# A software-pipelined attention pass on one Trainium2 core: a new written order of the first pass, and the mixture's weights fetched one piece per element

## The reference, cut to what matters

```python
x = x + _L0_xattn_ref(_layernorm(x), ctx, ctx, mask, ...)   # 16 heads of 8, 77 keys, bias by distance
x = x + _L0_ffn_ref(_layernorm(x), ...)                      # the two parts below
# part 1: layer norm, 3-tap convolution over tokens, q k v, rotation of q and k,
#         causal attention with 16 heads over 128 keys, projection
# part 2: layer norm, h @ router_w, argmax over 4 experts, then for the chosen expert
#         (silu(gate) * value) @ expert_proj[e], with gate, value = split(h @ expert_wv[e])
```

## Time and profile before

| what | us |
|---|---|
| time, three runs | 3200.71, 3202.42, 3205.06 |
| median | 3202.42 |
| the profiled execution, its own time | 3210.65 |
| its span, first to last instruction | 3208.9 |
| busy in the span: PE, DVE, ACT, POOL | 2783.6, 2658.8, 2508.3, 828.6 |

### The profile page before, as it was taken

How to read it: one execution, slowest core, us unless ns; L and a number is a source line. 1 busy time by engine, 2 the same in 40 slices (tenths; PEclk the granted TensorE clock), 3 DMA queues, 4 the chain that set the end, 5 groups by cost and what they waited for, 6 DMA issues and landing times. The chain is left out here.

```text
span 3208.9 us, 78310 instructions
## 1 busy us (share of the span) xinstructions
PE 2783.6 (87%) x28057; PEld 2002.6 (62%) x28057; DVE 2658.8 (83%) x7379; ACT 2508.3 (78%) x6617; POOL 828.6 (26%) x1437
## 2 busy tenths in 40 slices
PE   6999899999999759979999997876688888888887
PEld 4666666666666536656767674334566667667665
DVE  4899898999989525459999995788599999999995
ACT  4999899999999525547777773687599998999995
POOL 1233233333333100025555541000122221222221
PEclk7999999999999669989999997998789998999997
DMA  1011311111111011101111111001200000000000
GB/s 47 26 33 33 78 33 33 33 30 31 32 33 33 14 54 42 43 22 33 35 34 35 34 33 30 1 0 32 69 10 15 15 15 15 14 15 15 15 15 8
DMA packets 176000, 91.15 MB, mean 28 GB/s; under 512 B 46243, under 2 KB 171877, under 8 KB 175619
## 3 DMA queue, kind: packets, MB, share of 16 engines
q1 hardware_dynamic: 170084, 76.85, 8.9%
q0 software_dynamic: 4096, 8.40, 0.8%
q10 hardware_dynamic: 1440, 0.90, 0.1%
HBM read 43.73 MB, written 42.36 MB: 27 GB/s over the span
## 5 line engine op out<-in xcount | busy, mean ns | idle before, releaser
L2299 DVE TENSOR_TENSOR th<-tf 128x2048 f32<-128x2048 f32 x256 | 583.5, 2279 | 12.1 <-PE p_rho L2203 8.1
L2149 ACT ACTIVATE th<-th 128x2048 f32<-128x2048 f32 x256 | 488.9, 1911 | 6.8 <-DVE th L2299 6.8
L643 ACT ACTIVATE probf<-probf,colf 128x128 f32<-128x128 f32 x1024 | 314.4, 403 | 0.0
L2203 PE MATMUL p_rho<-th,late_w_row 128*32 128x128 f32 x8192 | 301.6, 285 | 13.1 <-ACT th L2149 13.1
L613 ACT ACTIVATE prob<-prob,col 128x77 f32<-128x77 f32 x1024 | 270.0, 352 | 4.6 <-DVE col L896 4.6
L2160 ACT ACTIVATE tl<-tf 128x128 f32<-128x128 f32 x832 | 256.9, 390 | 0.0
L2203 PEld LDWEIGHTS p_rho<-th,late_w_row 128*32 128x32 f32 x8192 | 229.4, 113 | 28.3 <-ACT th L2149 17.8
L1755 PE MATMUL acc<-xnT_all,wT 128*128 128x512 f32 x384 | 181.3, 625 | 29.6 <-DVE tmax L1947 13.2
L791 PE MATMUL fp<-ident,probf 128*128 128x128 f32 x1024 | 145.0, 287 | 27.3 <-ACT ygf L650 24.6
L942 DVE TENSOR_TENSOR probf<-fs,causal 128x1024 f32<-128x1024 f32 x128 | 153.7, 1201 | 16.9 <-PE fs L779 16.9
L2264 PE MATMUL p_f<-w_pair,xm 128*128 128x128 f32 x1024 | 166.8, 330 | 0.0
(11 more groups left out here) (432 smaller groups left out, 7964.2 us busy)
## 6 DMA issues: line engine op xcount, KB each, us to landing
rows<-zeros SPq DMA_DIRECT2D x64, 256.0 KB, 2.4
cxT<-in_ctxT SPq DMA_DIRECT2D x128, 38.5 KB, 2.0
xb<-rows SPq DMA_DIRECT2D x67, 64.0 KB, 1.8
rows<-yb SPq DMA_DIRECT2D x67, 64.0 KB, 1.5
x<-in_x SPq DMA_DIRECT2D x64, 64.0 KB, 1.8
x_mid<-x SPq DMA_DIRECT2D x64, 64.0 KB, 1.5
z<-x_mid SPq DMA_DIRECT2D x64, 64.0 KB
x_next<-z SPq DMA_DIRECT2D x64, 64.0 KB, 1.5
```

What stands on the lines that cost most here:

```text
L643: last = nc.scalar.activation(scores, scores, ACT.Exp, bias=colf[s][:, 16 + HALF * hf + h:17 + HALF * hf + h])
L2149: nc.scalar.activation(b[:], b[:], ACT.Tanh).then_inc(act_done, ACT_L.did(f"t{c}.tanh", e))
L2203: last = nc.tensor.matmul(p_rho[r][ROWS * b:ROWS * (b + 1), 0:TOK], w_row[:, ROWS - 1 - a:2 * ROWS - 1 - a], tanh[:, k, :], start=(a == 0) ...
L2299: nc.vector.tensor_tensor(th[i % NT][:], tf[s][:, n * KT:(n + 1) * KT].unsqueeze(2).to_broadcast([128, KT, TOK]), tf[s][:, FEAT:FEAT + TOK ...
```

## The change

The four texts of the first pass are replaced. The steps and what they compute stay; only their order on each engine and the number of turns by which each lags are new. The first lines of the diff show all of the new PE, ACT, DVE and POOL orders.

Beside it the two transfers of all four experts' weights become four and four, one per expert, and SP no longer issues the list at e = 16 but one entry of it per element, from e = 8 on: 13 entries of `moe_loads` at e = 8 to 20 and the four convolution rows at e = 21 to 24.

```diff
+PE_A = """
+    x0b.PT@2 f0a.PV@5 f0b.S@4 f0b.PT@5 f0.qkv@3 x0b.PV@2 f0b.PV@5 x0.T x0.ygT@2 f0.ygT@5 x0.qkv fc.route@6 f0.yT@5
+    x0.yT@2 f0.o@5 x0.o@2 x0a.S x0a.PT@1 fc.rank@6 fc.T@5 f0a.S@3 x0b.S x0a.PV@1 f0a.PT@4 f0.T@2
+"""
 ACT_A = """
-    f0a.exp@5 x0.v@1 fc.xT@6 x0a.PTc@2 f0a.PTc@5 x0a.yg@2 f0b.exp@5 f0a.yg@5 f0.xT@3 x0b.PTc@2 f0b.PTc@5 x0a.exp@1
-    f0b.yg@5 x0b.yg@2 x0b.exp@1 f0.yT@5 f0.v@3 x0.xT x0.yT@2
+    f0b.yg@5 x0.xT x0a.exp@1 f0.yT@5 x0.yT@2 x0.v f0a.exp@4 x0a.PTc@1 fc.xT@5 f0b.exp@4 x0a.yg@1 f0a.PTc@4 f0.xT@2
+    x0b.PTc@1 f0a.yg@4 x0b.exp f0b.PTc@4 x0b.yg@1 f0.v@2
 """
 DVE_A = """
-    fc.eq@7 fc.first@7 f0.x@6 fc.stats@6 fc.aggr@6 x0.x@3 fc.eps@6 fc.pick@7 fc.taken@7 x0.kT@1 f0.stats@3 f0.aggr@3
-    fc.norm@6 x0.qT@1 f0.qk@4 f0.eps@3 f0b.max@5 x0a.add@1 f0.h@3 fc.slot@7 x0a.max@1 f0.norm@3 x0b.add@1 f0a.add@4
-    x0b.max@1 f0.conv2@3 f0.conv1@3 x0.stats f0.conv0@3 f0a.max@4 x0.aggr f0b.add@4 x0.eps f0.rope@3 f0.rden@5 f0.y@5
-    x0.rden@2 x0.norm x0.y@2 fc.slot_i@7 fc.max@6
-"""
-PE_A = """
-    x0b.S@1 f0a.S@4 f0a.PV@5 f0.T@3 x0b.PT@2 f0b.PT@5 f0b.S@4 x0b.PV@2 f0b.PV@5 f0.qkv@3 f0.ygT@5 x0.ygT@2 fc.route@6
-    f0.yT@5 x0.T x0.yT@2 f0.o@5 x0.o@2 x0.qkv x0a.PT@1 fc.rank@6 fc.T@5 x0a.S f0a.PT@4 x0a.PV@1
+    f0b.max@5 x0.rden@3 f0.rden@6 f0.y@6 x0.y@3 x0.kT@1 fc.max@7 x0.qT@1 fc.eq@7 f0.qk@4 f0.x@6 fc.first@7 fc.stats@6
+    x0.x@3 fc.aggr@6 fc.eps@6 f0.stats@3 f0.aggr@3 fc.pick@7 f0.eps@3 fc.taken@7 fc.norm@6 fc.slot@7 fc.slot_i@7
+    f0.h@3 x0a.add@1 f0.norm@3 x0a.max@1 x0b.add@1 f0a.add@4 x0b.max@1 f0a.max@4 f0.conv2@3 f0.conv1@3 f0.conv0@3
+    f0b.add@4 x0.stats x0.aggr x0.eps f0.rope@3 x0.norm
 """
 POOL_A = """
-    f0.rstd@3 x0.rstd fc.scatter@7 fc.rstd@5 x0.kblk fc.z@5 f0.kblk@3
+    fc.scatter@7 fc.z@6 x0.rstd x0.kblk f0.kblk@3 fc.rstd@5 f0.rstd@2
 """
...
-            (w_gv.rearrange("p (e n) -> p e n", e=MOE0), d["L0_ffn_expert_wv"].rearrange("e c n -> c e n")),
-            (w_dn.rearrange("p (e k n) -> p e k n", e=MOE0, k=CHUNKS0), d["L0_ffn_expert_proj"].rearrange("e (k c) n -> c e k n", c=CH)),
+            *((w_gv[:, i * 2 * FF0:(i + 1) * 2 * FF0], d["L0_ffn_expert_wv"][i, :, :]) for i in range(MOE0)),
+            *((w_dn[:, i * FF0:(i + 1) * FF0].rearrange("p (k n) -> p k n", k=CHUNKS0), d["L0_ffn_expert_proj"][i, :, :].rearrange("(k c) n -> c k n", c=CH)) for i in range(MOE0)),
...
             for e in range(BATCH):
-                if e == BATCH // 4:
-                    for dst, src in moe_loads:
-                        sp.dma_start(dst, src).then_inc(moe_in, 16)
-                    for tap in range(4):
-                        sp.dma_start(conv1_rows[tap:tap + 1, :]...).then_inc(moe_in, 16)
+                n = e - BATCH // 8
+                if 0 <= n < len(moe_loads):
+                    sp.dma_start(moe_loads[n][0], moe_loads[n][1]).then_inc(moe_in, 16)
+                elif 0 <= n - len(moe_loads) < 4:
+                    tap = n - len(moe_loads)
+                    sp.dma_start(conv1_rows[tap:tap + 1, :]...).then_inc(moe_in, 16)
                 if e + CLEAR_AHEAD < BATCH:
                     clear(e + CLEAR_AHEAD)
                 store(e)
```

More of the change, by code:

```diff
@@ L521, in _ @@
             for e in range(BATCH):
-                if e == BATCH // 4:
-                    for dst, src in moe_loads:
-                        sp.dma_start(dst, src).then_inc(moe_in, 16)
-                    for tap in range(4):
-                        sp.dma_start(conv1_rows[tap:tap + 1, :].rearrange("j (k p) -> p k j", p=CH), d["L1_ffn_conv"][:, :, tap:tap + 1], allow_slow_non_contiguous=True).then_inc(moe_in, 16)
+                n = e - BATCH // 8
[3 more added lines that the diff above has]
+                    tap = n - len(moe_loads)
+                    sp.dma_start(conv1_rows[tap:tap + 1, :].rearrange("j (k p) -> p k j", p=CH), d["L1_ffn_conv"][:, :, tap:tap + 1], allow_slow_non_contiguous=True).then_inc(moe_in, 16)
                 if e + CLEAR_AHEAD < BATCH:
```

## The result

The changed kernel takes 3191.03 us (median of 11 runs, 3179.26 to 3197.02), the one before 3200.71 in the runs beside it (11 runs, 3195.46 to 3205.51). The ratio is 0.9965, 95% interval 0.995 to 0.9979: 0.35% faster. The forecast was 3164 us, with a range from 3147 to 3184, so it was wrong: of the 38.9 us forecast, about 10 arrived.

What follows compares the result with a forecast made beforehand. The prediction took each turn as ACT's work plus two waits for PE, 16.18 us. Savings of 28.4 (turns), 7.5 (input wait) and 3 (end of pass), 38.9 us in all, gave 3164 us, range 3147 to 3184.

Steps and rivals of the forecast that it cites:

- The turn: First pass: from 16.18 to 15.69 us, ACT's work 15.15 plus holes of 0.41 and 0.13; 28.4 us saved over 58 turns.
- ties: Rival: late steps of PE and ACT add up, turn 16.0 to 16.18 us, time 3185 to 3195; chance 0.13.
- PE as the bound: Rival: PE loses the overlap and keeps its idle time, turn 16.68 us, time 3224, slower; chance 0.06.
- returned overlap: Rival: the two `S` overlap again and holes are short, turn 15.3 to 15.5 us, about 3146; chance 0.08.
- `x0b.S` behind `f0a.S` without overlap: On PE, `x0b.S` comes second and waits for `x0a.add`; PE's work grows by up to 0.5 us a turn, hidden.
- All at a granted clock of 1.00: First pass, old order: PE, ACT and DVE near full at once, with TensorE at its 2.4 GHz level.
- the work of each engine stays: Per turn, ACT, PE and DVE stay at 15.15, 15.10 and 14.60 us, except where neighbours overlapped.
- The wait goes, 7.5 us: DVE's single 7.91 us wait for an input behind the experts' weights disappears, at a net gain of 7.5 us.
- what could remain ... mostly inside the slack of 0.8: Inputs landing 0 to 1 us late in the 8 turns with a large weight piece, mostly within DVE's 0.8 us slack.
- the pieces don't help: Rival: each turn's weight piece makes the input late, 8 x 1 us, cancelling the stall's gain; time 3171, chance 0.03.
- Elements 0 to 5: Start of the first pass: the few turns before element 5 are set by latency; no gain or loss counted.
- The end of the pass, 3 us: From `x0.stats` of element 63 to its `fc.slot_i`: 3 us saved, between -3 and 6, as `f0b.add` comes earlier.

Runs made afterwards that it cites:

- e4: The changed kernel run once more with no edit, for a second trace: 3189.78 us (one run).
- e5: The changed kernel with all weight pieces and convolution rows issued in element 0's turn: 3178.1 us, ratio 0.9912.
- e6: e5 plus two full 128 x 128 transposes of the identity on TensorE ahead of `f0a.S`: 3166.44 us, ratio 0.9885.
- e11: The changed kernel with its own transfers, plus two full 128 x 128 transposes ahead of `f0a.S`: 3170.09 us, ratio 0.9913.
- e12: e6 run once more, for a second trace: 3165.34 us (one run).
- e7: e5 plus two full transposes put ahead of the wait for `f0.yT`, where PE otherwise idles: 3175.51 us (3 runs), ratio 0.992.
- e10: e6 with one narrow matmul (32 rows) in place of the two transposes: lower than the expected 3175 us; exact time not given.
- e8: The old orders with weights and rows issued at element 0 as in e5, and `x0a.PV`'s matmuls issued twice: 3197.16 us, ratio 0.9977.
- e2: The kernel before with its old orders, but the weights in pieces, one transfer per element: 3195.25 us, ratio 0.9972.
- e3: The changed kernel with the four convolution rows issued at elements 0 to 3: 3177.99 us, ratio 0.9932.

## Why the prediction was wrong, step by step

- **The turn: right.** 15.69 us forecast, 15.69 to 15.70 measured in all ten traces of new orders. Its two chains: from the start of `f0b.PTc` to that of `f0b.yg` 1.75 forecast, 568.58 to 570.35 = 1.77 measured; from `x0a.yg` to `x0b.PTc` 1.66 forecast, 579.32 to 581.10 = 1.78 measured (timeline of ACT):

```profile
568.58 1.00 ACT L648 COPY probTf<-fp 128x1024 f32<-128x1024 f32 x1
...
570.35 0.38 ACT L651 COPY ygf<-fp 128x256 f32<-128x256 f32 x1
...
579.32 0.35 ACT L621 COPY yg<-xp 128x256 f32<-128x256 f32 x1
...
581.10 1.00 ACT L618 COPY probT<-xp 77x1024 f32<-77x1024 f32 x1
```

  The holes in them are not where they were forecast. In the first chain ACT is idle for 0.12 us before `x0b.yg` and 0.10 before `f0b.yg`, where one of 0.41 was forecast; before `x0b.PTc` it is not idle at all, but for 0.17 before `f0a.PTc`. ACT's idle time is 15.69 - 15.27 = 0.42 us a turn, not 0.54, and its work 15.27, not 15.15: two errors of 0.12 that cancel, so that the exact 15.69 is in part luck. The rivals of ties, of PE as the bound and of a returned overlap are out.
- **`x0b.S` behind `f0a.S` without overlap: right.** 576.16 + 1.13 = 577.29, and `x0b.S` starts at 577.28 (PE's timeline of an undisturbed turn); `x0a.add`, for which it waits, ends at 577.23:

```profile
576.16 1.13 PE L780 MATMUL fs<-kblkf,qTf 32*128 32x512 f32 x4
577.28 0.79 PE L725 MATMUL xs<-kblk,qT 32*128 32x308 f32 x4
```

  The rule of the Trainium skill weighed in the prediction ("TensorE: Matmul & The Clock Gate", Part 3, "Packing small matmuls — row/col tiling") thus gave nothing for this pair, since the second of it has a wait of its own.
- **"All at a granted clock of 1.00", and "the work of each engine stays": failed.** The old level of the clock was taken over into an order whose PE list had been changed. The prediction even named the new neighbours, `f0a.S`, `x0b.S` and `x0a.PV`, and priced their overlap only, not the clock. The cost is 6.9 us in the profiled execution (5 falls), 17.7 in e4's (13) and 13.6 in e5's (10); e6, e11 and e12 take it away, and e7 and e10 show that neither the same work in another place nor narrow work in the same place does so.
- **"The wait goes, 7.5 us", and "what could remain ... mostly inside the slack of 0.8": failed in the new order.** The four rows of 4-byte pieces were counted as bytes. The Trainium skill ("DMA: Bandwidth & Descriptors", section "Why small descriptors are slow (HBM only)") has a fixed cost in each packet that bytes don't show. The trace agrees that the pieces matter: a landing after 7.7 us in place of 2.0. No run shows that this fixed cost is the reason, and the load's own packets were in time. Of the 5.7 us that it was late DVE waited 3.60, and with the clock's stay at half behind it this became 9.5 us (4.8 in e4). With the unexplained stop before it, 16.9 us of long turns stand where 7.5 us of stall went. e5 has none of them.
- **The rival "the pieces don't help"** came true in effect, by another mechanism: the rows did it, not the large pieces, and it was given 0.03.
- **Elements 0 to 5, "I count nothing for them": most likely failed.** This stretch is 4.9 us longer in the profiled execution, and 72.0 to 77.0 us in the ten traces of new orders against 66.7 to 73.7 in the four of old ones (means 74.7 and 69.8). The same kernel had 76.7 and 72.8, so the size is uncertain, and which step causes it is not shown.
- **The end of the pass, 3 us: mis-sized, in its bounds.** It gave 5.6; the old orders take 98.6 to 103.5 us there, the new ones 94.4 to 97.9. In the profiled execution it returns about what elements 0 to 5 lose.
- **The difference of the profiled execution to the median**, 8 us before and 5 after, is not explained. The traces show one place where executions differ: behind the pass, in stages that no edit here touches, they take 2064.4 to 2073.0 us, 2072.9 of them in the trace before.

With both losses gone the time comes near the forecast: e6, 3166.44 us, and e12, 3165.34, against 3164. From `x0.stats` of element 0 to the last `fc.slot_i` they take 1085.2 and 1080.6 us, where the kernel before takes 1121.0: 35.8 and 40.4 off, with 38.9 forecast. Of these the 58 turns give 32.6 and 34.0, with 35.9 forecast. That the sum fits so well is in part luck: the gain at the end of the pass was larger than forecast, and elements 0 to 5 took some of it back. So the order is worth about what was read off; what was missed is mostly the clock and the rows.

What stays open: why 2.87 us of narrow work in the old order (e8) bring no fall, so that the length of the stretch doesn't decide (the full step ahead of it is one candidate, which no run takes away), and why falls come in some turns and not in others of the same order, often in several turns running; which loads a row delays (4 of the 15 with a row right behind them in the new order, none of 4 in e2, which may be chance); the stop at 443 us, which one trace of the changed kernel has and the other has not. Times of single theories within 5 us (e5, e7, e10) are not told apart by the runs, only their falls are.

## What to carry to other kernels

A new order of TensorE's list is to be read for the clock as well as for waits: look for the place where narrow steps have lost the full-width step ahead of them, compare the granted clock behind it, and try a full-width matmul there. Take more than one trace: one kernel had 5 falls in one and 13 in the other. Count a transfer beside a latency-bound load by its pieces, not by its bytes, and issue it where nothing waits. A wait of a few us on a full TensorE is priced with the stretch at half clock behind it: 3.6 us became 9.5 in one trace here and 4.8 in another.

## What the runs showed of the hardware

- The granted clock falls to 1.2 GHz, for 3.4 us, while TensorE is busy with hardly a pause (0.03 to 0.46 us idle in the 4 us ahead), 45 times in the 406 turns of the new order without the added transposes, always at the end of the narrow stretch (7 in `x0a.PV`, 38 in `f0a.PT` behind it). Two added 128 x 128 transposes (0.38 us) ahead of the stretch leave 1 such fall in 174 turns. The Trainium skill ("TensorE: Matmul & The Clock Gate", Part 1, "HAM oscillation — how this bites in real kernels") puts such falls down to gaps in TensorE's work; here e10's row of 505.98 has it busy for 3.96 of the 4 us ahead of one, so that rule alone would not find them.
- How long the clock stays low behind a stop varies widely, even in one kernel: 17.1 us behind DVE's wait of 3.60 (changed kernel), 3.4 behind one of 3.67 (e4). Behind a wait of 7.91 us it was low from 366.6 to 373.4 with the old order, behind 9.63 us from 365.6 to 389.5 with the new one, though PE was busy for 7.74 of 8 us from 374 on. Whether the order has a part in this is not shown.
- Of the 15 loads of `ctxT` that have a transfer of 512 pieces of 4 bytes issued right behind them in the new order (after, e3, e4, e11), 4 land after 7.7 to 9.1 us, the others after 1.8 to 3.2. The data of the late ones arrive within 2.9 us; the notice of their landing comes only near the end of the 4-byte packets.
